# Attention scores in four groups of 32 array rows, and the best logit subtracted once instead of per tile

## The chip, the cores and the metric

The kernel runs on one core of one Trainium2 chip. The metric is device time in microseconds (us) of one execution. TensorE (PE) multiplies matrices, VectorE (DVE) and ScalarE (ACT) read its results from PSUM, GpSimd (POOL) works on SBUF and issues indirect DMAs, and SyncE (SP) issues the other DMAs. The engines run side by side and wait for each other by semaphores.

## The reference, cut to what matters

Two layers work on x of shape (2, 1024, 256) in float32. Each is an attention over a context of 77 rows, then a feed-forward part with experts. Both attentions have 16 heads of depth 16. In layer 0 the router keeps the four best of 32 experts for a token, and weights them by a softmax over their logits:

```python
q = _split_heads(x @ Wq.T) * DEPTH ** (-0.5)
k = _split_heads(y @ Wk.T)
v = _split_heads(y @ Wv.T)
logits = jnp.einsum('bhqd,bhkd->bhqk', q, k) + bias
weights = jax.nn.softmax(logits, axis=-1)
attn = jnp.einsum('bhqk,bhkd->bhqd', weights, v)
...
logits = flat.astype(jnp.float32) @ router_w.T + router_bias
scores = jax.nn.softmax(logits, axis=-1)
topk_scores, topk_idx = jax.lax.top_k(scores, TOPK)
topk_scores = topk_scores / jnp.clip(topk_scores.sum(axis=-1, keepdims=True), 1e-12, None)
```

In layer 1 a mask takes the place of the bias, there are biases on q, k, v and the output, and the router takes the one best of 8 experts.

## The kernel before, in words

The 2048 tokens are 16 tiles of 128. Each layer goes through an attention stage (one pipelined loop over the tiles, with the router of the same layer woven in) and an expert stage. Layer 0 has a shared expert between them (12 tiles after the attention, the other four inside layer 1's attention), then 95 gathered tiles of 128 rows (`experts0`); layer 1 has 23 gathered tiles (`experts1`).

The attention loop is written out by hand. Every engine has its own function `step(t)` for t from -5 on, and a step handles several tiles at different depths: `on(t, 2)` guards the work on tile t+2, and so on. On PE a step (`step0`, `step1`) is, in layer 0: transpose the first half of the softmax numerators (`transpose_p`, L885), router logits of tile t-2 (L907), output projection of tile t-1 (L914), turn the normalised rows of tile t+2 (`rows_turned`, L900), the other transposes (L885, L892, L893), the queries of tile t+2 (L923), the weighted values of tile t (`weigh`, L937: ten blocks, 51 columns each), **the scores of tile t+2 (`scores`, L950)**, turn the router's rows (L959), turn the attention's output (L966). A float32 matmul of the program appears in the trace as two LDWEIGHTS and two MATMULs. Layer 1 has the same parts in another order.

`scores` makes the logits of 16 heads against 77 context rows. The keys lie block-diagonal in `kbd`: a group of 64 array rows holds 4 heads of 16 rows, against 4 x 77 = 308 columns, so that one matmul with 64 rows (half the array) makes 4 heads. Four matmuls, g = 0 to 3, go to banks 0 to 3; g even uses rows 0 to 63 and g odd rows 64 to 127. `kbd` is filled on DVE (`keys`, L1433) from the keys times `mask_k`.

DVE's order in a step is written by hand as well. For layer 0: add the router's bias (L1535), maximum over the keys for heads 8 to 15 of tile t+1 (`maxima`, L1497), the 8 best logits of tile t-2 (`dve.max`, L1543), residual add (L1506), their indices (L1553), statistics for two layer norms (L1397), **the four best logits minus the best into `wgt` (L1565)**, mean and variance (L1402), indices to float (`ef`, L1579), one-hot of the four experts of tile t-3 and two sums (`chosen0`, L1458, L1462, L1464), epsilon (L1406), reciprocal of the softmax sum (L1597), normalised output (`o_sb`, L1599), the two layer norms (`xr`, `xn`, L1410), four additions of the bias to the scores in banks 0 to 3 (L1626), maxima of heads 0 to 7 (L1497). In layer 1 four multiply-adds that combine layer 0's expert rows (`combine`, L1488) stand in between, and L1565 and `chosen0` do not exist; L1574, L1584 and L1609 rank the tokens of an expert.

POOL in a step computes 1/sqrt for both norms (L585, L590); in layer 0 it subtracts the maxima from a whole tile of scores (L609), in layer 1 it gathers expert rows (L597) and adds the output bias (L604). ACT copies transposes to SBUF (L683, L720, L721, L708, L698, L743), scales the queries (L726, L730) and takes the exponentials (L736 for a whole tile in layer 0, L691 head by head in layer 1). Behind `experts0` ACT takes the exponential of all of `wgt` (L807) after a wait on the semaphore `RT["below"]`. `keep_busy` (L844) issues matmuls on ones that nobody reads.

```python
for g in range(NG):
    pe.wait_ge(T["q"], n + 3)
    if g % 2 == 0:
        need(pe, T["copied"], 2 * n + 3 + g // 2)
...
    dve.tensor_scalar(wgt[:, bass.ds((t - 2) * TOPK, TOPK)], m8[w][:, 0:TOPK], m8[w][:, 0:1],
                      None, ALU.subtract).then_inc(RT["below"], 1)
```

Of the kernel before, what the change touches and what calls it, by code (L numbers as in the profile page):

```python
# [22 lines left out]
P = 128  # L23
# [10 lines left out]
HG = 4  # L34
NG = H // HG
PC = (H * S2 + P - 1) // P
LASTROWS = H * S2 - (PC - 1) * P
# [20 lines left out]
NOH = NT  # L58
TEMP_END = 9276
VF_BACK = 632  # L60


def need(eng, sem, n):

    if not isinstance(n, int) or n > 0:
        eng.wait_ge(sem, n)
# [13 lines left out]
def build(nc, A):  # L80
    ctx = ExitStack()
    with ctx:
# [6 lines left out]
        def cut(region, at, shape, dt=F32):  # L89

            n = int(np.prod(shape))
            words = n if dt in (F32, I32, U32) else (n + 1) // 2
            v = region[:, at:at + words]
            if dt != F32:
                v = v.bitcast(dt)
            if len(shape) > 1:
                names = "abcd"[:len(shape)]
                v = v.rearrange(f"p ({' '.join(names)}) -> p {' '.join(names)}",
                                **dict(zip(names, shape)))
            return v, at + words  # L100
# [25 lines left out]
        kbd, vbd, bias = [None, None], [None, None], [None, None]  # L126
        kbd[0], o = cut(R2, o, (B * KC, HG, S2))
        vbd[0], o = cut(R2, o, (B * PC, 3 * VC))
# [6 lines left out]
        for name in ("Wq", "Wk", "Wv", "Wo"):  # L135
            attn_w[1][name], o = cut(U, o, (KC, D))
        kbd[1], o = cut(U, o, (B * KC, HG, S2))
        vbd[1], o = cut(U, o, (B * PC, 3 * VC))
# [84 lines left out]
        own_e, tile_less, tok_1 = route1[:, 0:E1], route1[:, E1:E1 + PLAN1], route1[:, E1 + PLAN1:]  # L223
        mask_k = sb("mask_k", [P, HG])
        mask_v = sb("mask_v", [P, PC, 3])
# [20 lines left out]
        lg = sb("lg", [P, E0])  # L246
        m8 = [sb(f"m8_{i}", [P, 8]) for i in range(2)]
        i8 = [sb(f"i8_{i}", [P, 8], U32) for i in range(2)]
        ef = sb("ef", [P, NT * TOPK])
# [414 lines left out]
        def _(act):  # L664
# [140 lines left out]
            experts0_steps(act, experts0)  # L805
            act.wait_ge(RT["below"], NT)
            act.activation(wgt[:, :], wgt[:, :], ACT.Exp).then_inc(R0["exp"], 1)  # L807
# [31 lines left out]
        def _(pe):  # L839
# [35 lines left out]
            def attention(l):  # L875
# [66 lines left out]
                def scores(t, n):  # L942

                    for g in range(NG):
                        pe.wait_ge(T["q"], n + 3)
                        if g % 2 == 0:
                            need(pe, T["copied"], 2 * n + 3 + g // 2)
                        c, half = g // 2, g % 2
                        r = slice(64 * half, 64 * half + 64)
                        mm = pe.matmul(bank[g][:, 0:HG * S2], qT[r, c, :],  # L950
                                       kbd[l][r, batch(t, 2) * KC + c].rearrange("p h k -> p (h k)"),
                                       start=True, stop=True)
                        if half:
                            mm.then_inc(T["sc_mm"], 1)

# [436 lines left out]
        def _(dve):  # L1392
# [29 lines left out]
            def keys(l):  # L1422
                K = KV
                dve.wait_ge(consts_in, 16 * CONSTS)
                for m in range(KC):
                    dve.wait_ge(K["k_mm"], 2 * KC if l else m + 1)
                    if m:
                        dve.wait_ge(K["k_bd"], B * (KC * l + m))
                    dve.tensor_scalar(k_sb, kv_k[l][m], bqk[:, 1, m:m + 1] if l else 0.0, None,
                                      ALU.add).then_inc(K["k_sb"], 1)  # L1430
                    dve.wait_ge(K["k_sb"], KC * l + m + 1)
                    for b in range(B):
                        dve.tensor_tensor(kbd[l][:, b * KC + m],  # L1433
                                          k_sb[:, b * S2:(b + 1) * S2].unsqueeze(1).to_broadcast([P, HG, S2]),
                                          mask_k[:, :].unsqueeze(2).to_broadcast([P, HG, S2]),
                                          ALU.mult).then_inc(K["k_bd"], 1)
# [29 lines left out]
            def attention(l):  # L1466
# [41 lines left out]
                def step(t):  # L1508
# [3 lines left out]
                    ne, nk = (E0, E1)[l], (TOPK, 1)[l]  # L1512
                    w, m = par(-2), n - 1
                    if l == 0 and isinstance(t, int) and t == -2:
                        keys(0)
                        dve.tensor_copy(iota16[:, :], iota[:, :])
                        dve.wait_ge(bias_in[0], 32)
                        dve.wait_ge(route_in[0], 32)
# [21 lines left out]
                    if on(t, -2):  # L1540

                        wait_apart(dve, RT["lg"], m)
                        dve.max(m8[w][:, :], lg[:, 0:ne]).then_inc(RT["mx"], 1)  # L1543
                    if l == 1 and on(t, -3):
# [6 lines left out]
                    if on(t, -2):  # L1551
                        wait_apart(dve, RT["mx"], m)
                        dve.max_index(i8[w][:, :], m8[w][:, :], lg[:, 0:ne]).then_inc(RT["ix"], 1)  # L1553
                    if l == 1 and on(t, 3):
# [4 lines left out]
                    if on(t, 3):  # L1559
                        if l == 1:  # L1560
                            wait_apart(dve, TL["x_comb"], t + 4)
                        row_stats(T, par(3), t + 3)
                    if l == 0 and on(t, -2):

                        dve.tensor_scalar(wgt[:, bass.ds((t - 2) * TOPK, TOPK)], m8[w][:, 0:TOPK], m8[w][:, 0:1],  # L1565
                                          None, ALU.subtract).then_inc(RT["below"], 1)
                    if on(t, -1):
# [3 lines left out]
                    if l == 1 and on(t, -3):  # L1571

                        dve.wait_ge(TL["rank"], t - 2)
                        dve.scalar_tensor_tensor(out=slot[:, bass.ds(t - 3, 1)], in0=ef[:, bass.ds(t - 3, 1)],  # L1574
                                                 scalar=float(N), in1=rk[:, 0:1], op0=ALU.mult,
                                                 op1=ALU.add).then_inc(TL["slot"], 1)
                    if on(t, -2):
                        dve.wait_ge(RT["ix"], m)
                        dve.tensor_copy(ef[:, bass.ds((t - 2) * nk, nk)], i8[w][:, 0:nk]).then_inc(RT["ef"], 1)  # L1579
                    if l == 0 and on(t, -3):  # L1580
                        chosen0(t - 3)
                    if l == 1 and on(t, -2):
# [383 lines left out]
            def experts0(s):  # L1966
                u = par(0)
                if isinstance(s, int) and s == 0:

                    dve.wait_ge(bias_in[1], 16)  # L1970
                    dve.tensor_scalar(bias[1], bias[1].bitcast(I32), 0.0, MASKED, ALU.is_equal,
                                      ALU.mult).then_inc(KV["mask"], 1)
# [48 lines left out]
def constants():  # L2021
# [4 lines left out]
        "ident": np.eye(P, dtype=np.float32),  # L2026
        "mask_k": ((p[:, None] % 64) // DH == np.arange(HG)).astype(np.float32),
        "mask_v": ((f // S2)[:, :, None] == (np.array(HEAD0)[None, :, None] + np.arange(3))).astype(np.float32)
# [53 lines left out]
```

## Time and profile before

| | |
|---|---|
| median of 3 runs | 785.07 us (783.95 to 786.47) |
| profiled execution | 784.07 us, its span 782.2 us (1.87 us lie around the span) |
| busy in the span | PE 729.4, PE weight loads 592.1, DVE 457.4, ACT 324.7, POOL 306.5 us |
| mean granted PE clock | 0.981 |
| attention of layer 0 | about 16 to 159 us |
| shared expert, experts0 | about 160 to 435 us |
| attention of layer 1 | about 435 to 590 us |
| experts1 | from about 597 us |

Times in a row are us from the span's start unless marked ns. In a row of a timeline, "x8" merges eight instructions of a line; the brackets at the end give how long the engine sat idle before it and who ended that. PEld is the weight load of PE, which overlaps its matmuls. The clock 1.00 is 2.4 GHz and 0.50 is 1.2 GHz.

### The profile page before, as it was taken

Reading aid. Unit: us, or ns where it says so; the run is one execution under the profiler, and the core shown is the slowest. Engines: PE = TensorE matmul, PEld = TensorE weight load, DVE = VectorE, ACT = ScalarE, POOL = GpSimd, SP = SyncE. Lnnn points to the kernel's source line nnn. Section 1 sums busy time; section 2 is a strip of 40 time slices with the busy share of each in tenths; the row PEclk is TensorE's granted clock in tenths of the full one; section 3 lists DMA queues with packets and bytes.
Section 4 is the critical chain, followed back from the end, with each engine's and each line's share of the span. In section 5 each row is a group of like instructions: output and inputs, shape, how many; then the busy total and the mean of one; then the engine's idle time right before and its main releaser. Section 6 shows DMA issues by size and latency. Waiting matters only on the chain.

```text
span 782.2 us, 15464 instructions
## 1 busy us (share of the span) xinstructions
PE 729.4 (93%) x4576; PEld 592.1 (76%) x4577; DVE 457.4 (58%) x1697; ACT 324.7 (42%) x1000; POOL 306.5 (39%) x331
## 2 busy tenths in 40 slices
PE   8799999999998999999999799988997999999994
PEld 4578888856665888888875488777774999999993
DVE  2689999647973544444433779999984232232331
ACT  1345555422221455555543488877850212212210
POOL 1243443300022555555514667763113244344421
PEclk9999999899999999999999999999998999999998
DMA  7423433340014455555872236776521565555530
GB/s 208 150 95 97 141 108 127 109 128 21 14 54 88 140 160 162 163 163 161 135 128 68 68 92 184 218 202 177 154 68 52 188 201 162 194 196 162 196 130 5
DMA packets 64181, 103.05 MB, mean 132 GB/s; under 512 B 20145, under 2 KB 42113, under 8 KB 63860
## 3 DMA queue, kind: packets, MB, share of 16 engines
q1 hardware_dynamic: 52852, 72.88, 29.9%
q0 software_dynamic: 10976, 27.22, 14.1%
q10 hardware_dynamic: 288, 2.10, 0.8%
q8 instruction: 39, 0.64, 0.3%
q14 instruction: 26, 0.21, 0.1%
HBM read 82.83 MB, written 22.07 MB: 134 GB/s over the span
## 4 chain that ended last, share of the span: by engine, by line
PE 64%; DVE 27%; DMA 3%; issue 2%; ACT 2%; POOL 1%; SPq 0%; DVEq 0%; ACTq 0%; POOLq 0%
PE bank L1368 11%; PE bank L1383 10%; PE bank L1316 9%; PE bank L937 5%; DVE U L1626 5%; PE bank L1329 5%; PE bank L1240 4%; DVE mx L1497 3%; DVE X L1488 2%; PE bank L844 2%; PE bank L1307 2%; PE bank L1288 2%; PE bank L923 2%; DMA expert_out<-U 2%; DVE R L1856 2%
## 5 line engine op out<-in xcount | busy, mean ns | idle before, releaser
L622 POOL DMA_INDIRECT U<-normed,idx_all x95 | 90.3, 951 | 141.8 <-PE bank L1307 73.7
L1316 PE MATMUL bank<-R,U 128*128 x380 | 99.2, 384 | 0.1
L1368 PE MATMUL bank<-X,R 128*128 128x128 f32 x736 | 85.9, 275 | 0.0
L1368 PEld LDWEIGHTS bank<-X,R 128*128 128x128 f32 x736 | 84.1, 192 | 0.1
L1383 PE MATMUL bank<-R,X 128*128 (+1 forms) x368 | 83.1, 379 | 0.0
L1977 DVE TENSOR_TENSOR U<-U,bank 128x128 f32<-128x128 f32 x95 | 27.3, 287 | 83.0 <-ACT U L804 82.9
L597 POOL DMA_INDIRECT R<-expert_out,slot x64 | 61.5, 960 | 35.1 <-DMA expert_out<-xr 17.7
L1383 PEld LDWEIGHTS bank<-R,X 128*128 128x128 f32 x368 | 68.2, 190 | 8.4
L691 ACT ACTIVATE U<-U,mx 128x77 f32<-128x77 f32 x256 | 67.3, 352 | 12.6 <-DVE mx L1497 12.6
L1316 PEld LDWEIGHTS bank<-R,U 128*128 128x128 f32 x380 | 65.4, 192 | 5.6 <-issue 0.3
L609 POOL TENSOR_TENSOR U<-U,mx 128x1232 f32<-128x1232 f32 x16 | 36.0, 2249 | 68.9 <-DVE mx L1497 68.9
L2005 DVE TENSOR_SCALAR X<-bank,U 128x128 f32<-128x128 f32 x92 | 25.9, 344 | 62.0 <-PE bank L1368 44.3
L648 POOL DMA_INDIRECT out<-U,idx_all x23 | 23.7, 1028 | 90.7 <-DVE U L2016 85.9
L1329 PE MATMUL bank<-R,U 128*128 x190 | 57.3, 385 | 0.1
L800 ACT ACTIVATE U<-bank 128x128 f32<-128x128 f32 x95 | 26.3, 277 | 60.7 <-PE bank L1323 60.7
L585 POOL TENSOR_TENSOR rstd<-ve,neg_half 128x1 f32<-128x1 f32 x32 | 18.1, 565 | 82.2 <-DVE ve L1406 82.2
L1497 DVE TENSOR_REDUCE mx<-U 128x8 f32<-128x616 f32 x64 | 49.9, 783 | 0.0
L820 ACT ACTIVATE X<-bank 128x256 f32<-128x256 f32 x23 | 8.8, 383 | 94.3 <-PE bank L1357 94.3
L796 ACT ACTIVATE U<-bank 128x256 f32<-128x256 f32 x95 | 36.4, 383 | 22.3 <-PE bank L1307 22.3
L1240 PE MATMUL bank<-R,xT 128*128 128x512 f32 x96 | 45.1, 593 | 0.0
L885 PE MATMUL bank<-ident,U 128*128 128x128 f32 x248 | 39.1, 283 | 4.5 <-ACT U L736 4.2
L683 ACT ACTIVATE U<-bank 128x512 f32<-128x512 f32 x62 | 36.9, 598 | 14.4 <-PE bank L885 11.5
(255 smaller groups left out, 1541.2 us busy)
## 6 DMA issues: line engine op xcount, KB each, us to landing
R<-in_w SPq DMA_DIRECT2D x21, 1024.0 KB
R<-in_w SPq DMA_DIRECT2D x40, 256.0 KB
R<-in_gu SPq DMA_DIRECT2D x8, 1024.0 KB, 5.8
expert_out<-U SPq DMA_DIRECT2D x48, 128.0 KB
expert_out<-xr SPq DMA_DIRECT2D x47, 128.0 KB
normed<-xr SPq DMA_DIRECT2D x32, 128.0 KB, 3.1
R<-in_down SPq DMA_DIRECT2D x8, 512.0 KB, 3.6
x<-X SPq DMA_DIRECT2D x16, 128.0 KB
```

Of the source, the lines that this page charges most:

```text
L597: pool.indirect_dma_start(yg[:, (i % NYG) * TOPK + j, :], None, y_d, bass.IndirectOffsetOnAxis(slot[:, a:a + 1], 0)).then_inc(TL["gath"][i ...
L622: pool.indirect_dma_start(xg0[i % NXG], None, xn_d[0], bass.IndirectOffsetOnAxis(idx_all[:, i:i + 1], 0)).then_inc(EX[0]["gath"][i % NXG], 16)
L691: ins = act.activation(sc[u][:, h * S2:(h + 1) * S2], sc[u][:, h * S2:(h + 1) * S2], ACT.Exp, bias=mx[u][:, h:h + 1])
L885: mm = pe.transpose(bank[5 + g][:, (c % 4) * P:(c % 4 + 1) * P], sc[u][:, c * P:(c + 1) * P], ident[:, :])
L937: mm = pe.matmul(bank[7][:, HEAD0[c] * VC:HEAD0[c] * VC + cols], pT[0:rows, c, :], vbd[l][0:rows, batch(t, 0) * PC + c, 0:cols], start=(c ...
L1240: mm = pe.matmul(bank[2 * v + a][:, :], xT_[:, c, :], sgu_w[:, c, a * FS:(a + 1) * FS], start=(c == 0), stop=(c == KC - 1))
L1316: mm = pe.matmul(bank[2 + u][:, 0:2 * F0], xgT0[u][:, c, :], gu_w[:, c, bass.ds(e, 1), :].rearrange("p a n -> p (a n)"), start=(c == 0), s ...
L1329: pe.matmul(bank[6 + u][:, 0:D], hT0[u], down_w[:, bass.ds(e, 1), :].rearrange("p a n -> p (a n)"), start=True, stop=True).then_inc(X0["dn ...
L1368: mm = pe.matmul(bank[1 + 2 * v + f // 4][:, (f % 4) * P:(f % 4 + 1) * P], w1_of[v][:, c, f * P:(f + 1) * P], xgT1[v][:, c, :], start=(c = ...
L1383: mm = pe.matmul(bank[6 + u][:, 0:D], hT1[u][:, c, :], w2_w[:, bass.ds(e, 1), c, :].rearrange("p a n -> p (a n)"), start=(c == 0), stop=(c ...
L1497: dve.tensor_reduce(mx[u][:, 8 * g:8 * g + 8], s3[:, 8 * g:8 * g + 8, :], AX.X, ALU.max, negate=(l == 1)).then_inc(T["mx"], 1)
L1626: ins = dve.tensor_tensor(s3[:, HG * q:HG * q + HG, :], bank[q][:, 0:HG * S2].rearrange("p (h k) -> p h k", h=HG), bt.to_broadcast([P, HG, ...
```

## The change

The scores of a tile are made by eight matmuls with 32 array rows each instead of four with 64. A group of 32 rows holds two heads, against 2 x 77 = 154 columns. The eight go in two rounds (c = 0, 1) of four groups (g = 0 to 3); group g writes bank g, round c its half of the 308 columns. Both increments of `sc_mm` now come in the last round. The rows of Wq and Wk (and their biases) are permuted on the host so that banks hold the same heads as before; `kbd` and `mask_k` have half the columns. `wgt` is no longer made tile by tile: `dve.max` of layer 0 writes into a buffer for all tiles (`best0`), and one subtraction over all 16 tiles stands at step 0 of `experts0`. In DVE's step `chosen0` stands ahead of the conversion of the indices.

```diff
+QH, QR = HG // KC, P // NG
...
-        kbd[0], o = cut(R2, o, (B * KC, HG, S2))
+        kbd[0], o = cut(R2, o, (B * KC, QH, S2))
...
+        best0 = sb("best0", [P, NT, 8])
...
-            act.wait_ge(RT["below"], NT)
+            act.wait_ge(RT["below"], 1)
             act.activation(wgt[:, :], wgt[:, :], ACT.Exp).then_inc(R0["exp"], 1)
...
-                    for g in range(NG):
-                        pe.wait_ge(T["q"], n + 3)
-                        if g % 2 == 0:
-                            need(pe, T["copied"], 2 * n + 3 + g // 2)
-                        c, half = g // 2, g % 2
-                        r = slice(64 * half, 64 * half + 64)
-                        mm = pe.matmul(bank[g][:, 0:HG * S2], qT[r, c, :],
-                                       kbd[l][r, batch(t, 2) * KC + c].rearrange("p h k -> p (h k)"),
-                                       start=True, stop=True)
-                        if half:
-                            mm.then_inc(T["sc_mm"], 1)
+                    pe.wait_ge(T["q"], n + 3)
+                    for c in range(KC):
+                        for g in range(NG):
+                            if c == 0 and g % 2 == 0:
+                                need(pe, T["copied"], 2 * n + 3 + g // 2)
+                            r = slice(QR * g, QR * g + QR)
+                            mm = pe.matmul(bank[g][:, c * QH * S2:(c + 1) * QH * S2], qT[r, c, :],
+                                           kbd[l][r, batch(t, 2) * KC + c].rearrange("p h k -> p (h k)"),
+                                           start=True, stop=True)
+                            if c == KC - 1 and g % 2:
+                                mm.then_inc(T["sc_mm"], 1)
...
+                    best = best0[:, min(max(t - 2, 0), NT - 1), :] if l == 0 else m8[w][:, :]
...
-                        dve.max(m8[w][:, :], lg[:, 0:ne]).then_inc(RT["mx"], 1)
+                        dve.max(best, lg[:, 0:ne]).then_inc(RT["mx"], 1)
...
-                    if l == 0 and on(t, -2):
-
-                        dve.tensor_scalar(wgt[:, bass.ds((t - 2) * TOPK, TOPK)], m8[w][:, 0:TOPK], m8[w][:, 0:1],
-                                          None, ALU.subtract).then_inc(RT["below"], 1)
...
+                    if l == 0 and on(t, -3):
+                        chosen0(t - 3)
                     if on(t, -2):
                         dve.wait_ge(RT["ix"], m)
                         dve.tensor_copy(ef[:, bass.ds((t - 2) * nk, nk)], i8[w][:, 0:nk]).then_inc(RT["ef"], 1)
-                    if l == 0 and on(t, -3):
-                        chosen0(t - 3)
...
                 if isinstance(s, int) and s == 0:

+                    dve.wait_ge(RT["mx"], NT)
+                    dve.tensor_tensor(wgt[:, :].rearrange("p (t j) -> p t j", t=NT), best0[:, :, 0:TOPK],
+                                      best0[:, :, 0:1].to_broadcast([P, NT, TOPK]), ALU.subtract).then_inc(RT["below"], 1)
...
-        "mask_k": ((p[:, None] % 64) // DH == np.arange(HG)).astype(np.float32),
+        "mask_k": ((p[:, None] % QR) // DH == np.arange(QH)).astype(np.float32),
```

## Rows read from the trace of the kernel before

**Rows 1.** The chain of waits in layer 0: start, us, engine and line.
```profile
87.80 0.44 PE bank L900 x2
...
93.43 1.54 DVE U L1626 x4
...
95.83 0.44 PE bank L900 x2
...
145.20 1.44 DVE wgt L1565
```

**Rows 2.** The timeline of one steady tile of layer 0.
```profile
88.53 2.25 POOL L609 TENSOR_TENSOR U<-U,mx 128x1232 f32<-128x1232 f32 x1 [3.71 <-DVE mx L1497]
...
89.61 1.19 DVE L1565 TENSOR_SCALAR wgt<-m 128x4 f32<-128x4 f32 x1
...
91.96 1.31 PE L950 MATMUL bank<-R,qT 64*128 64x308 f32 x8
92.07 0.26 DVE L1597 RECIPROCAL rs<-bank 128x16 f32<-128x16 f32 x1 [0.31 <-PE bank L937]
...
93.20 0.44 PE L959 MATMUL bank<-ident,xr 128*128 128x128 f32 x2
```

**Rows 3.** Busy in layer 1's attention: PE, PEld, DVE, ACT, POOL, clock, DMA, GB/s.
```profile
470.00:560.00 90.00, 82.69 (x633) 69.91 (x632) 88.51 (x339) 71.75 (x256) 51.92 (x65) 1.00 0.66 190
```

**Rows 4.** L950 alone in slices of that tile: slice, its length, PE (x) and PEld (x).
```profile
91.95:91.97 0.02, 0.01 (x2) 0.01 (x2) 1.00 0.00 0
91.97:92.30 0.33, 0.33 (x2) 0.29 (x4) 1.00 0.00 0
```

**Rows 5.** The view and columns of rows 3, two stretches at the end of layer 0's attention.
```profile
144.80:148.10 3.30, 2.38 (x20) 2.26 (x20) 3.18 (x11) 1.64 (x4) 2.35 (x2) 1.00 0.54 218
148.20:155.00 6.80, 6.31 (x26) 5.82 (x27) 2.47 (x14) 2.25 (x6) 0.00 (x0) 0.50 0.45 135
```

**Rows 6.** The timeline at the start of layer 1's attention.
```profile
445.24 2.43 PE L950 MATMUL bank<-U,qT 64*128 64x308 f32 x8 [3.78 <-ACT qT L730]
...
447.60 3.66 PE L844 MATMUL bank<-ones 128*128 128x512 bf16 x14
...
456.17 0.26 DVE L1597 RECIPROCAL rs<-bank 128x16 f32<-128x16 f32 x1 [3.87 <-PE bank L937]
```

**Rows 7.** The timeline at the last scores of layer 1.
```profile
569.27 1.31 PE L950 MATMUL bank<-U,qT 64*128 64x308 f32 x8
...
569.67 0.42 DVE L1599 TENSOR_TENSOR o_sb<-bank,rs 128x256 f32<-128x256 f32 x1
...
570.51 0.44 PE L966 MATMUL bank<-ident,o_sb 128*128 128x128 f32 x2
...
573.60 0.17 DVE L1529 TENSOR_TENSOR U<-bank,U 128x8 f32<-128x8 f32 x1 [0.86 <-PE bank L914]
```

**Rows 8.** The timeline at the end of layer 0's attention.
```profile
145.12 1.52 DVE L1565 TENSOR_SCALAR wgt<-m 128x4 f32<-128x4 f32 x1
...
148.69 0.69 PE L959 MATMUL bank<-ident,xr 128*128 128x128 f32 x2 [1.51 <-DVE xr L1410]
...
151.17 2.05 PE L914 MATMUL bank<-R,oT 128*128 128x256 f32 x4
...
161.45 0.21 DVE L1565 TENSOR_SCALAR wgt<-m 128x4 f32<-128x4 f32 x1
```

**Rows 9.** The timeline of a steady tile of layer 1.
```profile
483.43 1.11 PE L914 MATMUL bank<-U,oT 128*128 128x256 f32 x4
...
484.76 0.16 DVE L1529 TENSOR_TENSOR U<-bank,U 128x8 f32<-128x8 f32 x1
...
487.42 0.74 POOL L604 TENSOR_TENSOR X<-X,U 128x256 f32<-128x256 f32 x1
...
487.88 0.32 DVE L1574 SCALAR_TENSOR_TENSOR slot<-ef,rk 128x1 int32<-128x1 f32 x1
```

**Rows 10.** The page: the costliest groups of instructions.
```profile
L1977 DVE TENSOR_TENSOR U<-U,bank 128x128 f32<-128x128 f32 x95 | 27.3, 287 | 83.0 <-ACT U L804 82.9
```

More of the change, by code:

```diff
@@ L58 @@
 NOH = NT
-TEMP_END = 9276
+TEMP_END = 8660
 VF_BACK = 632
@@ L136, in build @@
             attn_w[1][name], o = cut(U, o, (KC, D))
-        kbd[1], o = cut(U, o, (B * KC, HG, S2))
+        kbd[1], o = cut(U, o, (B * KC, QH, S2))
         vbd[1], o = cut(U, o, (B * PC, 3 * VC))
@@ L223, in build @@
         own_e, tile_less, tok_1 = route1[:, 0:E1], route1[:, E1:E1 + PLAN1], route1[:, E1 + PLAN1:]
-        mask_k = sb("mask_k", [P, HG])
+        mask_k = sb("mask_k", [P, QH])
         mask_v = sb("mask_v", [P, PC, 3])
@@ L1433, in keys @@
                         dve.tensor_tensor(kbd[l][:, b * KC + m],
-                                          k_sb[:, b * S2:(b + 1) * S2].unsqueeze(1).to_broadcast([P, HG, S2]),
-                                          mask_k[:, :].unsqueeze(2).to_broadcast([P, HG, S2]),
+                                          k_sb[:, b * S2:(b + 1) * S2].unsqueeze(1).to_broadcast([P, QH, S2]),
+                                          mask_k[:, :].unsqueeze(2).to_broadcast([P, QH, S2]),
                                           ALU.mult).then_inc(K["k_bd"], 1)
@@ L1552, in step @@
                         wait_apart(dve, RT["mx"], m)
-                        dve.max_index(i8[w][:, :], m8[w][:, :], lg[:, 0:ne]).then_inc(RT["ix"], 1)
+                        dve.max_index(i8[w][:, :], best, lg[:, 0:ne]).then_inc(RT["ix"], 1)
                     if l == 1 and on(t, 3):
@@ L2052 @@
     arrays["ctxT"] = rows_of(a["ctx_1024"].reshape(B * S2, D).T)
+    rows = np.arange(D).reshape(NG, KC, QH * DH).swapaxes(0, 1).reshape(D)
     for l in range(2):
         for w in ("Wq", "Wk", "Wv", "Wo"):
-            arrays[f"L{l}_{w}"] = rows_of(a[f"L{l}_xattn_{w}"].T)
+            m = a[f"L{l}_xattn_{w}"]
+            arrays[f"L{l}_{w}"] = rows_of((m[rows] if w in ("Wq", "Wk") else m).T)
     arrays["bias0"] = rows_of(a["fside_1x1xSxS2_0"].reshape(S, S2))
     arrays["mask1"] = rows_of(a["mask_BxSxS2_if1"].reshape(N, S2))
-    arrays["bqk"] = np.stack([a["L1_xattn_bq"].reshape(KC, P).T, a["L1_xattn_bk"].reshape(KC, P).T], 1)
+    arrays["bqk"] = np.stack([a["L1_xattn_bq"][rows].reshape(KC, P).T, a["L1_xattn_bk"][rows].reshape(KC, P).T], 1)
     arrays["bv"] = a["L1_xattn_bv"].reshape(1, D)
```

## The prediction

> **What bounds the kernel now.** The change touches three things: PE's scores (L950), a small subtraction on DVE (L1565), and the place of a conversion. Whether their time counts depends on the stage, so I read the chain of waits first, then the timeline around each place.
>
> In the attention of layer 0 a tile takes 95.83 - 87.80 = 8.03 us, and two engines share it in series [rows 1]. PE has it from its turned rows at 87.80 to the end of the weighted values at about 92.04. DVE has it from its reciprocal at 92.07 [rows 2] to 95.8: output, two norms, four additions to the scores (93.43), the maxima, the router's bias, which frees PE again. The scores are on neither half. They start at 91.96, behind the values, and PE then idles until DVE has made `xr`, so that L959 starts only at 93.20 [rows 2]. In PE's half DVE has 0.31 us to spare ahead of its reciprocal, although L1565 takes 1.19 us there [rows 2]. In layer 1's steady tiles DVE is busy 88.51 us of 90 and the chain runs on DVE alone [rows 3].
>
> **Scores on PE.** One tile is eight trace matmuls in 1.31 us [rows 2]. They go in pairs, one per row group: in the first 0.02 us two weight loads and two matmuls start, and then no further matmul until 92.30 [rows 4]. From the first start, 0.36 us pass to the second pair; four pairs and the run-out fill 1.31, so a later pair takes about 0.26 us, which fits 308 columns. A weight load of 128 columns goes at 2.26/20 = 0.113 us when they follow each other over all rows [rows 5]. After the change there are sixteen matmuls of 154 columns in four rounds of four. If the four groups overlap as the two do now, a round costs the larger of 0.13 (half of 0.26) and 0.113 us: an estimate of 0.10 (first load) + 4 x 0.13 + 0.26 (run-out) = 0.8 to 0.9 us, that is 0.5 us less for PE in a tile. From below: with no overlap beyond today's two groups it would stay at 1.3; with loads one behind the other it is dearer (a rival below).
>
> The Trainium skill ("TensorE: Matmul & The Clock Gate", Part 3) says that weight loads overlap running matmuls only where the row group differs, and that four 32-row groups gave 3.07 times the speed of one; on its rule the sixteen would end within my estimate. The trace agrees for two groups [rows 4], and no row shows four.
>
> What do the 0.5 us bring? In layer 0's steady tiles nothing: PE waits for `xr` anyway. Both releases of DVE's additions now come with the last round, at about 91.96 + 0.85 = 92.8, still ahead of the first addition at 93.4 [rows 1]. In layer 1's steady tiles nothing, for DVE is the chain. Two tiles are different.
> - The second scores of layer 1 (445.24) take 2.43 us against 1.31, as at half clock; 14 `keep_busy` matmuls of 3.66 us follow and then the first transposes [rows 6]. Half clock doubles my rounds: 0.1 + 4 x 0.26 + 0.1 = 1.2 us, so PE is 1.2 us earlier. Of that, keep-busy matmuls give back 0.4, because I estimate that two more of them fall into the half-clock time (14 took 3.66 us, 0.26 each over both clocks). DVE idles 3.87 us in front of the first reciprocal (456.17), so the shift reaches it: **-0.75** (bounds 0 and -1.2).
> - The last scores (569.27) hold up L966, whose input is there at 569.67 + 0.42 = 570.09, but which starts at 570.51. PE is the bound from there, since DVE idles 0.86 us for it at 573.60 [rows 7]: **-0.4** (bounds 0 and -0.42).
>
> The first scores of each layer are released by ACT and release DVE; their first half took 0.8 us and all of them will: 0 (bounds -0.1, +0.1). The new order waits for `copied` a little earlier, but DVE copied those banks a tile before: 0. The four multiplications of `keys` halve; they lie ahead of the first scores and off the chain: 0.
>
> **The subtraction.** L1565 costs 0.21 us where POOL is quiet (161.45) and 1.52 us at 145.12 [rows 8]. In the steady tile it ends at 89.61 + 1.19 = 90.80, and POOL's L609 ends at 88.53 + 2.25 = 90.78 [rows 2]: DVE waits there for POOL. Removing it takes 1.2 to 1.5 us of DVE time from each tile in which it meets POOL, and 0.2 from the last ones. In the steady tiles that lengthens a wait of 0.31 us that PE ends: 0. On the chain it stands once, at tile step 14: 1.44 us at 145.20 [rows 1], where no scores follow, and from there through `ve`, POOL and `xr` to L959 at 148.69, in front of which PE idled 1.51 us [rows 8].
>
> What is late next there? DVE's next operation is the one-hot of `chosen0`, moved ahead of the conversion. It has two SBUF inputs. A row says that such an operation waits for POOL too: L1574 takes 0.32 us and ends at 488.20, just after L604 at 487.42 + 0.74 = 488.16 [rows 9]. So the stall moves on to L1458, and what is left to gain is the end of L1565, L1402 and the two small ones that now run inside the wait: **-0.3**. If L1458 is not held, its three operations (0.7 us) run during POOL's and the conversion takes the stall: -0.6, the lower bound; the upper is 0.
>
> The Trainium skill ("SBUF — State Buffer", "Who interferes with whom") says that a VectorE instruction with two SBUF inputs contends with a GpSimd instruction that reads SBUF. It speaks against the move: by it the term is -0.3, without it -0.6. The row on L1574 agrees.
>
> At step 17 the subtraction is on the way to the router's counts: **-0.1**. The one subtraction in `experts0` is 64 elements wide, a fraction of a microsecond, in a stage where DVE idles 83 us in front of L1977 [rows 10]: 0, and at most +0.3 if that cover were gone. Its added wait on `RT["mx"]` is over long before, and what queues behind it (the mask, values of layer 1) is not needed at once. ACT's wait on `below` comes after `experts0`: 0.
>
> **Sum**: -0.75 - 0.4 - 0.3 - 0.1 = -1.55 us, from 784.07 to 782.5 for the profiled execution, whose time is 1.0 below the median. Against the median of 785.07: **783.5 us**, -0.2%. All bounds together give -2.4 to +0.4, so 782.7 to 785.5.
>
> **The rivals.**
> 1. *The clock falls in layer 1 (slower).* At 144.8 to 148.1 PE did 19 of the narrow matmuls of L937 and then idled, 2.38 us busy of 3.30; from 148.2 to 155.0 the granted clock was 0.50 (1.2 GHz) [rows 5]. The steady part of layer 1 held 1.00 [rows 3]. Its tiles have the same 20 narrow matmuls, then 1.31 us of wide scores, then short idle times. The scores shrink to 0.85 and the idle time grows, so this place comes nearer to the one where the clock fell. Price: behind it PE has 12 turns and transposes until L914. At half clock two took 0.69 instead of 0.44 us [rows 2, 8], so 12 lose 1.5; L914 takes 2.05 instead of 1.11 [rows 8, 9], 0.9 more. The margin ahead of DVE's L1529 is 484.76 - 484.54 = 0.2 [rows 9]. That is 2.2 us if all of it is hit, 1.4 if two thirds are. It decides from the third fall on (3 x 1.4 - 1.55 = +2.65). For three to six falls: 787.7 to 791.9, with four 789.1. Against it: PE is idle 7.3 us of 90 there already, and the clock held [rows 3]. Chance 0.20; one or two falls (784.9 to 786.3) 0.10.
> 2. *The fall at the end of layer 0 goes away (faster).* `xr` comes 0.3 to 0.6 us earlier and the idle gap of 1.51 us shrinks. If the 6.8 us of 1.2 GHz [rows 5] vanish, PE's work there (6.31 us) loses at most 3.2 us; with 2.5, as L937 is bound by weight loads, 781.0. For it: the gap sits just there. Against it: it only shrinks, and the narrow matmuls stay. Chance 0.14.
> 3. *Four groups do not load together.* Sixteen loads in series cost 16 x 0.113 = 1.8 us [rows 5], 2.05 with the run-out: DVE's additions in layer 0 would start 0.65 us later in some 15 tiles, +10 us, 793.5 and more. Rows 4 speak against it. If so, each load here is as dear as a full one. Chance 0.04.
> 4. *The edge terms come to nothing* (PE's lead is taken up by ACT at 451 or by DVE at 570): 785.1. Chance 0.06.
>
> **How the numbers follow.** The forecast has 0.46. The point from which a measurement can tell a change is 0.3%, 2.4 us, about the spread of the three runs. Faster than 782.7: rival 2 and the lower edge of my bounds, 0.26. Slower than 787.4: rivals 1 (three falls or more) and 3, 0.24. Within: 0.50. The range of 781.0 to 788.5 reaches to rival 2 and takes in one to three falls; the forecast's own is 782.7 to 785.5.
>
> **What would show it.** L950 as x16 of 154 columns in 0.8 to 0.9 us, four starts within some 0.02 us; steady tiles of 8.0 and 8.5 us as before; L1597's idle in layer 0 longer; L1458 taking about 1 us beside L609, and so DVE's busy time in layer 0 down by only about half of what L1565 took; L959 of step 14 about 0.3 us nearer to its predecessor; the clock 1.00 from 470 to 560. I am wrong if a steady tile of either layer changes by over 0.1 us, if L1458 takes 0.28 us beside L609, or if the granted clock in layer 1 shows a new fall.

## The result, and the profile after

The changed kernel takes **792.29 us** (790.06 to 797.09, four executions), the kernel before 785.46 (783.95 to 786.47, four executions): a ratio of **1.0095** with a 95% interval of **[1.0052, 1.0137]**. It is slower by 0.95%, and the interval does not reach 1. The prediction of 783.5 us is wrong, and so is its range of 781.0 to 788.5. The profiled execution took 790.06 us, its span is 788.2 us, and the mean granted clock fell from 0.981 to 0.961.

The page of the changed kernel: busy time of the engines. Most lines of the file lie two higher than before (L950 is L952 now, L966 is L968, L1458 is L1460); behind the place of L1565 some lie one lower (L1597 is L1596, L1626 is L1625).

```profile
PE 726.3 (92%) x4825; PEld 600.6 (76%) x4833; DVE 451.4 (57%) x1682; ACT 325.6 (41%) x1000; POOL 306.7 (39%) x331
```

PE and DVE are busy for 3 and 6 us less, and the time is longer. So some stretch has work that got slower or waits that got longer. First a steady tile of layer 0, from its timeline:

```profile
89.97 2.25 POOL L611 TENSOR_TENSOR U<-U,mx 128x1232 f32<-128x1232 f32 x1 [3.91 <-DVE mx L1499]
...
91.26 1.10 DVE L1460 TENSOR_TENSOR U<-iota,ef 128x128 bf16<-128x128 f32 x1
...
93.40 0.81 PE L952 MATMUL bank<-R,qT 32*128 32x154 f32 x16
...
93.50 0.26 DVE L1596 RECIPROCAL rs<-bank 128x16 f32<-128x16 f32 x1 [0.51 <-PE bank L939]
...
94.60 0.44 PE L961 MATMUL bank<-ident,xr 128*128 128x128 f32 x2 [0.39 <-DVE xr L1412]
```

It is as predicted: the scores take 0.81 us instead of 1.31, the stall beside POOL has gone from the subtraction to the one-hot (L1460 ends at 91.26 + 1.10 = 92.36, POOL at 89.97 + 2.25 = 92.22; compare [rows 2]), DVE's wait for PE is longer, and the tile takes 94.60 - 86.58 = 8.02 us from one L961 to the next, as before.

The loss is in the attention of layer 1. The starts of its scores, tile after tile, show where. This table is made from the timelines of both; a row is the time from one start to the next.

| from the 2nd scores of layer 1 | before, us | after, us |
|---|---|---|
| start of the 2nd scores | 445.24 | 442.87 |
| the next six starts, together | 51.14 (to 496.38) | 51.14 (to 494.01) |
| the next eight, one by one | 8.46, 9.23, 9.32, 9.02, 9.55, 9.15, 9.09, 9.07 | 8.59, 10.76, 9.92, 11.65, 8.32, 12.18, 8.32, 12.12 |
| those eight together | 72.89 | **81.86** |
| from the last scores to the end of the span | 212.9 | 212.3 |

-2.37 + 0 + 8.97 - 0.6 = +6.0 us: the whole difference of the two spans. (The -2.37 lies ahead of layer 1; at most 1.7 of it is a stretch of 3.4 us at clock 0.50 at 254 us, in PE's own stage, which this execution did not have.) And this is the clock, by windows: PE, PEld, DVE, ACT, POOL, clock, DMA share, GB/s. The kernel before, in the stretch of its eight tiles:

```profile
494.00:570.00 76.00, 68.07 (x523) 57.75 (x524) 74.24 (x291) 60.70 (x217) 35.73 (x47) 1.00 0.64 184
```

The changed kernel, in its own eight and over the stretch of [rows 3]:

```profile
470.00:560.00 90.00, 80.89 (x653) 72.19 (x654) 81.69 (x315) 67.12 (x233) 49.79 (x62) 0.89 0.62 180
...
494.00:576.00 82.00, 72.87 (x565) 65.76 (x567) 70.25 (x280) 59.03 (x207) 33.80 (x45) 0.83 0.56 161
```

The granted clock was 0.50 (1.2 GHz) in five stretches there: from 505.2 and 515.4 for 3.4 us, from 525.7, 546.1 and 566.6 for 6.8 us, 27.2 us in all. They cost 8.97 us, 1.8 each, or 0.33 us for each us at 1.2 GHz. By the table, the two short ones cost 1.53 and 0.60 us; the three long ones cost 6.7 us together, 2.2 each, if the shorter tile behind two of them is counted in.

**What a fall does.** A tile with one, in the timeline of the changed kernel:

```profile
546.30 1.06 PE L887 MATMUL bank<-ident,U 128*128 128x128 f32 x4
...
547.58 1.06 PE L887 MATMUL bank<-ident,U 128*128 128x128 f32 x4
...
548.53 1.00 PE L909 MATMUL bank<-rw,xrT 128*128 128x8 f32 x4
...
549.39 2.05 PE L916 MATMUL bank<-U,oT 128*128 128x256 f32 x4
...
551.55 0.17 DVE L1532 TENSOR_TENSOR U<-bank,U 128x8 f32<-128x8 f32 x1 [2.22 <-PE bank L916]
```

At 2.4 GHz these four groups take 0.60, 0.60, 0.59 and 1.11 us (the same kernel, from 487.67 on). DVE, which in the kernel before never waited for PE between 470 and 560 us ([rows 9]: L914 ended 0.2 us ahead of L1529), now waits 2.22 us for it, and that is the loss.

**What goes before one.** The first fall, at 505.2. PE and DVE in the timeline of the changed kernel:

```profile
494.01 0.81 PE L952 MATMUL bank<-U,qT 32*128 32x154 f32 x16
...
495.35 0.44 PE L968 MATMUL bank<-ident,o_sb 128*128 128x128 f32 x2 [0.53 <-DVE o_sb L1598]
...
500.25 2.42 PE L939 MATMUL bank<-U 128*128 128x51 f32 x20
...
502.60 0.81 PE L952 MATMUL bank<-U,qT 32*128 32x154 f32 x16
...
504.13 0.33 DVE L1883 TENSOR_SCALAR R<-iota,U,route 128x128 bf16<-128x128 bf16 x1
...
505.47 0.69 PE L968 MATMUL bank<-ident,o_sb 128*128 128x128 f32 x2 [2.06 <-DVE o_sb L1598]
```

The same step of the kernel before:

```profile
504.84 1.31 PE L950 MATMUL bank<-U,qT 64*128 64x308 f32 x8
507.30 0.44 PE L966 MATMUL bank<-ident,o_sb 128*128 128x128 f32 x2 [1.15 <-DVE o_sb L1599]
```

Layer 1 has two sorts of tiles. In the kernel before, a tile between 456 and 505 us is 8.46 us long or less. From the scores at 504.84 on DVE also works on the plan of `experts1` (L1884 and its neighbours, L1883 in the changed kernel), a tile takes 9.0 to 9.5 us, and PE idles longer behind its scores: 1.15 us before, and 2.06 us now. 2.42 us of narrow matmuls, 0.81 us of scores, 2.06 us of idle time: this is nearly the picture of [rows 5], ahead of the fall that the kernel before had at 148.2.

**The Trainium skill** ("TensorE: Matmul & The Clock Gate", the section on HAM oscillation) tells of gaps between the matmuls, in which TensorE waits for a DMA, as what lets the clock drop again and again in a kernel. The trace agrees in part. Here the wait is for DVE, and a gap alone does not settle it: the second fall of the changed kernel, at 515.4, comes beside a gap of 1.04 us, and the kernel before held its clock with gaps of 1.15 and 1.25. Nor is the harder sort of tile needed. A second execution of the changed kernel (e12 below) has its first fall of the steady tiles already at 499.4, beside the same gap of 0.53 us with which the one above held its clock at 495.35:

```profile
499.59 0.69 PE L968 MATMUL bank<-ident,o_sb 128*128 128x128 f32 x2 [0.53 <-DVE o_sb L1598]
```

So the picture ahead of 505.2 is one case of a fall. What decides in which tile a fall comes stays open.

### The profile page after: what moved, and what is told of

The parts are those of the page before. It is cut to its first block, busy times and chain, and to the rows that moved or that the text cites. A ratio compares the mean times of both kernels' runs of the same rounds, so it can differ in the third digit from the quotient of the medians.

```text
span 788.2 us, 15923 instructions
## 1 busy us (share of the span) xinstructions
PE 726.3 (92%) x4825; PEld 600.6 (76%) x4833; DVE 451.4 (57%) x1682; ACT 325.6 (41%) x1000; POOL 306.7 (39%) x331
## 4 chain that ended last, share of the span: by engine, by line
PE 61%; DVE 29%; DMA 2%; issue 2%; POOL 2%; ACT 2%; SPq 0%; DVEq 0%; ACTq 0%; POOLq 0%
PE bank L1370 10%; PE bank L1385 10%; PE bank L1318 10%; PE bank L1331 5%; PE bank L1242 4%; DVE U L1625 4%; DVE mx L1499 4%; PE bank L846 3%; PE bank L1309 2%; PE bank L939 2%; PE bank L1290 2%; PE bank L887 2%; DVE X L1490 2%; DVE stat L1399 2%; DVE R L1855 2%
## 5 line engine op out<-in xcount | busy, mean ns | idle before, releaser
L887 PE MATMUL bank<-ident,U 128*128 128x128 f32 x248 | 43.5, 306 | 4.9 <-ACT U L738 4.0
```

The costliest lines, as they stand in the source:

```text
L887: mm = pe.transpose(bank[5 + g][:, (c % 4) * P:(c % 4 + 1) * P], sc[u][:, c * P:(c + 1) * P], ident[:, :])
```

## The experiments

**The theories.** T1: the scores are shorter, PE works less and idles more in each tile of layer 1, and so the clock falls. T2: the form of the matmuls (32 rows, four groups) lets it fall, whatever their time. T3: the part on DVE does, or has a share. T4: the 0.95% is scatter. 18 runs were made. They fell on two kinds of chips, and this has to be told first: on kind A the kernel before takes 785.3 and 786.0 us, close to the 785.5 above; on kind B it takes 798.3 to 801.1. Each result stands beside the kernel before on its own chip.

| run | chip | median us | ratio to before [interval] | mean clock (before) |
|---|---|---|---|---|
| e12 changed | A | 794.67 | 1.0126 [1.0074, 1.0179] | 0.955 (0.974) |
| e9 changed, 4 fillers | A | 784.73 | 0.9991 [0.9964, 1.0018] | 0.977 (0.974) |
| e10 changed, 2 fillers and two edges | A | 784.26 | 0.9991 [0.9962, 1.0020] | 0.976 (0.974) |
| e11 before with the fillers of e10 | A | 784.59 | 1.0010 [0.9978, 1.0042] | 0.981 (0.974) |
| e17 before, half of layer 1's scores | A | 790.10 | 1.0065 [1.0033, 1.0098] | 0.960 (0.975) |
| e18 changed, scores twice | A | 787.27 | 1.0014 [0.9988, 1.0040] | 0.976 (0.975) |
| e5 before | B | 799.41 | 0.9981 [0.9943, 1.0018] | 0.968 (0.966) |
| e6 changed | B | 802.31 | 1.0029 [0.9997, 1.0060] | 0.952 (0.966) |
| e2, e16 changed, without the part on DVE | B | 803.96, 804.96 | 1.0055 [0.9999, 1.0110], 1.0054 [1.0023, 1.0085] | 0.949 (0.967), 0.945 (0.964) |
| e1, e15 before, with the part on DVE alone | B | 798.71, 802.09 | 0.9999 [0.9930, 1.0067], 1.0007 [0.9977, 1.0037] | 0.965 (0.967), 0.963 (0.964) |
| e4, e8 changed, 2 fillers | B | 798.39, 798.95 | 0.9999 [0.9934, 1.0063], 0.9988 [0.9952, 1.0024] | 0.964 (0.967), 0.965 (0.966) |
| e7, e14 before, half of layer 1's scores | B | 800.85, 800.88 | 1.0011 [0.9979, 1.0044], 0.9999 [0.9968, 1.0030] | 0.953 (0.966), 0.953 (0.964) |
| e3, e13 changed, scores twice | B | 827.66, 825.42 | 1.0369 [1.0306, 1.0432], 1.0308 [1.0242, 1.0374] | 0.943 (0.967), 0.947 (0.964) |

**Is it real (e12, e6).** The changed kernel once more, without an edit. e12:

> The changed kernel, unchanged, as the control of this call. T1: 0.3 to 1.0% above the kernel before, as in the two comparisons so far, with the mean granted clock 0.01 to 0.02 below that of the kernel before. T4 (scatter): a ratio of 1.000.

e6, on a chip of kind B:

> The changed kernel, unchanged, as a control on the same chip. T1 (less activity of PE in each tile of layer 1 lets the clock fall): 0.5 to 1.0% slower than the kernel before on this chip too, with three or more new stretches of 0.50 between 470 and 560 us. Rival T4 (the 1.0095 was scatter between executions, as falls come and go in either kernel): a ratio of about 1.000.

e12 has six stretches of 0.50 from 499.4 to 574.5 us, 27 us in all, and 1.0126: T4 is out on kind A. On kind B the time is 0.3% longer with an interval that takes in 1, below the 0.5 to 1.0% that T1 expected; the clock drops all the same, from 0.966 to 0.952 (on kind A from 0.974 to 0.955). So on kind B a loss of time is not shown for the whole change.

**The part on DVE alone (e1, e15), and the scores alone (e2, e16).** e1 is the kernel before with

```diff
+                    best = best0[:, min(max(t - 2, 0), NT - 1), :] if l == 0 else m8[w][:, :]
...
-                    if l == 0 and on(t, -2):
-                        dve.tensor_scalar(wgt[:, bass.ds((t - 2) * TOPK, TOPK)], m8[w][:, 0:TOPK], m8[w][:, 0:1], ...
...
+                    if l == 0 and on(t, -3):
+                        chosen0(t - 3)
...
+                    dve.tensor_tensor(wgt[:, :].rearrange("p (t j) -> p t j", t=NT), best0[:, :, 0:TOPK], ...
```

and e2 is the changed kernel with these lines undone.

> The kernel before with the part on DVE alone: best0, one subtraction in experts0, chosen0 ahead of the conversion; scores by four matmuls of 64 rows as before. T1 (the shorter scores leave PE less active in each tile of layer 1, and the granted clock falls there): the clock is 1.00 in layer 1's attention between 470 and 560 us as before; the time is that of before, less the 0.4 us of the prediction's terms for step 14 and 17, so 784.5 to 785.5. T3 (the moved stall on DVE brings the falls about): falls in layer 1 and 790 or more.

> The changed kernel with the part on DVE undone: four groups of 32 rows for the scores, the subtraction tile by tile as before. T1: the clock falls in layer 1's attention as in the changed kernel, 790 to 797. T3: no falls, about 784.

> The kernel before with the part on DVE alone. T1: the ratio to the kernel before lies at 1.000 with no stretch of 0.50 between 470 and 560 us; of the predicted 0.3 us at step 14 of layer 0 only 0.1 comes. T3 (the part on DVE has a share in the falls): a mean clock below 0.970 and 2 us or more.

> The changed kernel with the part on DVE undone. T1: all of the change's loss, 8 to 11 us more than the kernel before and a mean clock of 0.955. T3: less than half of that loss.

All four ran on kind B, where the kernel before has falls in layer 1 itself, so the absolute times of the expectations don't apply. The ratios do: the part on DVE alone makes no difference in time or clock (1.0007, 0.963 to 0.964), the scores alone give 1.0055 and 1.0054, and the clock falls to 0.949 and 0.945. T3 is out there. The part on DVE was not run alone on kind A, but e17 below has falls in layer 1 without it.

**Old form, half the time (e7, e14, e17).**

```diff
+                        wide = HG * S2 // (1, 2)[l]
-                        mm = pe.matmul(bank[g][:, 0:HG * S2], qT[r, c, :],
+                        mm = pe.matmul(bank[g][:, 0:wide], qT[r, c, :],
```

> The kernel before, with its four score matmuls of 64 rows, but in layer 1 over 154 of the 308 columns of each bank. It leaves out half of layer 1's scores (two heads of each bank). T1: PE's scores last 0.7 us instead of 1.3, as in the changed kernel, so falls of the clock appear between 470 and 560 us, and it takes as long as the changed kernel, 3 to 8 us more than the kernel before although it does less. T2 (four groups of 32 rows are the cause, not the shorter time): the time of the kernel before, or 1 us less.

> The kernel before with half of layer 1's scores left out (two heads of each bank), its matmuls over 64 rows, once more for the same reason. T1: stretches of 0.50 every 10 us between 470 and 560 us, and 5 to 10 us more than the kernel before. T2: no new stretches, the time of the kernel before or 0.5 us less.

> The kernel before with half of layer 1's scores left out (two heads of each bank), hoped for on a chip of the first kind, where the kernel before takes 785 us. T1: stretches of 0.50 every 10 us between 470 and 560 us, and 4 to 10 us more than the kernel before on such a chip. T2: the time of the kernel before or less. On a chip of the other kind (800 us): again a clock near 0.952 at an unchanged time.

**New form, twice the time (e3, e13, e18).**

```diff
-                    for c in range(KC):
+                    for c, again in ((0, 0), (0, 1), (1, 0), (1, 1)):
```

with the increments on the last of the four.

> The changed kernel with each of the eight score matmuls issued twice (a round with c=0 twice, then c=1 twice), so that PE spends about what the scores took before (1.3 to 1.5 us) in the same form of four groups of 32 rows. T1: no falls between 470 and 560, 783.5 to 786. T2 (matmuls on four groups of 32 rows do not count as activity whatever their time): the falls stay, 790 or more, and the time is above that of the changed kernel if anything.

> The changed kernel with each of its eight score matmuls issued twice, once more, since the first comparison ran on a chip with extra waits of its own in layer 1. T1 (PE's activity in a tile decides, whatever its form): no stretch of 0.50 between 470 and 560 us, a mean clock of 0.97 to 0.98 and the time of the kernel before, +0 to +1.5 us. T2 (matmuls on four groups of 32 rows don't hold the clock): falls as in the changed kernel, 0.955, and 8 to 11 us more than before.

> The changed kernel with each score matmul issued twice, hoped for on a chip of the first kind. T1: no stretch of 0.50 between 470 and 560 us, 0 to 1.5 us more than the kernel before. T2: falls as in the changed kernel, 8 to 11 us more. On a chip of the other kind: again about 25 us more, from PE's late results, which tells nothing between T1 and T2.

On kind A the pair answers T2. First e17, by lines of PE from 470 to 560 us (busy, mean ns of one | idle before) and by windows:

```profile
L951 PE MATMUL bank<-U,qT 64*128 64x154 f32 x72 | 7.2, 317 | 0.0
```

```profile
470.00:560.00 90.00, 80.92 (x580) 72.08 (x581) 82.37 (x315) 67.88 (x236) 49.62 (x62) 0.88 0.62 183
```

Then e18, the same two views:

```profile
L952 PE MATMUL bank<-U,qT 32*128 32x154 f32 x320 | 13.3, 302 | 0.0
```

```profile
470.00:560.00 90.00, 82.87 (x860) 74.17 (x859) 86.84 (x334) 70.87 (x250) 53.78 (x67) 0.98 0.64 188
```

The old form with half of its work left out is 0.65% slower than the whole, with a first fall at 505.2, the place of the changed kernel's. The new form with its work done twice is not measurably slower than before, has one fall of 3.4 us (519.5) where the changed kernel has 27 us, and stands nearer to the kernel before than the one that does it once (1.0014 against 1.0095 and 1.0126, which ran in other comparisons of kind A). So the form of the matmuls is neither needed for the falls nor enough for them, and what counts is how long the scores take: T2 is out. Two details are less clean than T1 had them. e17 has four stretches (from 505.2, 515.4, 535.9 and 556.4 us), not one every 10 us. e18 takes 1.3 us more than before, as T1 allows, but T1 had no stretch at all; its gap at 510.06 was still 1.55 us.

What these runs do not separate is the time that PE works and the time that it idles: whatever shortens the scores lengthens the gap behind them, and T1 takes the two as one.

On kind B neither tells this. e7 has a fall every 10.3 us from 471.6 to 577.4 us, as T1 says, but no loss; e3 and e13 lose 29 and 24 us, beside waits of another kind, which grow there (below).

**Give the activity back (e4, e8, e9).** In layer 1, behind the scores, k matmuls on ones into bank 4 that nobody reads; k = 2 in e4 and e8, 4 in e9:

```diff
+                    if on(t, 2) and on(t, 0):
+                        keep_busy(k, 4)
                     if t == -1:
                         keep_busy(14)
```

> The changed kernel with two keep_busy matmuls (128 rows, 512 columns, 0.43 us together at full clock) behind the scores of each tile of layer 1, where PE idles. T1: the activity that the scores lost is given back, the clock stays at 1.00 between 470 and 560, 783 to 785.5, which is not slower than before. T2: the falls have to do with the form of the scores and not with the idle time behind them, so they stay: 790 or more.

> The changed kernel with two keep_busy matmuls behind the scores of each tile of layer 1, beside its controls on one chip. T1: no new stretches of 0.50 between 470 and 560 us; the time of the kernel before or up to 1.5 us less. T2: the time of the changed kernel.

> The changed kernel with four keep_busy matmuls (0.85 us at full clock) behind the scores of each tile of layer 1 instead of two. T1 (PE's activity in a tile decides): at least as few stretches of 0.50 between 470 and 560 us as with two fillers and a mean granted clock of 0.96 to 0.98; the time of the run with two fillers or up to 1 us more, because at half clock the four take 1.7 us and then stand in front of the turn of o_sb. T2: the clock of the changed kernel, 0.95.

On kind B two fillers bring the mean clock from 0.952 (e6) to 0.965, and the ratio from 1.0029 to 0.9988; the two intervals overlap. The falls do not go away there, as T1 had expected: e4 has four and e8 has three stretches of 0.50 between 470 and 560 us, where the kernel before has two (e5) and the changed kernel five (e6). On kind A four fillers take the whole loss back: 784.73 us beside 794.67 of e12 on the same chip. By windows of e9, and in its timeline at the step that had the first fall:

```profile
470.00:560.00 90.00, 83.80 (x732) 70.97 (x741) 88.35 (x336) 70.28 (x248) 51.45 (x64) 1.00 0.64 187
```

```profile
508.15 0.44 PE L968 MATMUL bank<-ident,o_sb 128*128 128x128 f32 x2 [0.83 <-DVE o_sb L1600]
```

The work is the same in the same form, PE does 8.2 us more for nothing in these 90 us, and the time is 10 us less. That is what T1 says, and T2 does not allow it.

**A better kernel (e10, e11).** Two fillers as above and, in layer 0,

```diff
+                        if t == NT - 2:
+                            pe.wait_ge(T["copied"], 2 * NT)
+                            keep_busy(6, 0)
```

and in layer 1 `keep_busy(14)` ahead of the scores of t = -2. e11 has the same on the kernel before.

> The changed kernel with two fillers behind the scores of each tile of layer 1, 14 more ahead of the second scores of layer 1 (where PE waits 4.3 us for qT) and 6 where PE waits for xr at step 14 of layer 0. T1: the falls at about 150 us and 440 us go too, and with them some 2 us each (an execution of the kernel before lost 0.36 us for every us at 0.50): 3 to 4 us less than with two fillers alone, about 0.4% below the kernel before on this chip. Rival: the fillers stand in the way when the clock is low already and nothing is won against two fillers alone.

> The kernel before with the same fillers at the same three places. T1: its own falls at about 148 us and 445 us go, 3 to 4 us less than the kernel before; whatever the changed scores are worth in themselves shows as the difference to the changed kernel with these fillers, 0.5 to 1 us. Rival: its PE has less room behind the longer scores, so the fillers cost more than they bring: 0 to 3 us more than before.

The fillers of `keep_busy(14)` missed the place that they were meant for: the scores of t = -2 are the first of layer 1, and PE's long wait is ahead of the second. In e10:

```profile
436.35 0.81 PE L952 MATMUL bank<-U,qT 32*128 32x154 f32 x16
...
443.02 1.41 PE L952 MATMUL bank<-U,qT 32*128 32x154 f32 x16 [3.86 <-ACT qT L732]
```

So that fall stayed in both. The one at 150 us did go, in both: in e11 the steps behind it take 153.88 - 147.32 = 6.56 us between two L959, where the kernel before takes 158.09 - 148.69 = 9.40. But single executions of e11 reach from 780.5 to 790.9 us, as falls come and go elsewhere, and no ratio is under 1 by more than its interval. e10 still has one fall of 6.8 us in the steady tiles (534.7), e11 has none. No version beats the kernel before measurably, and the 3 to 4 us that were expected did not show.

**The kernel before on kind B (e5).**

> The kernel before, unchanged, as a control with its own trace: the last comparison ran on a chip where the kernel before took 798 us instead of 785, and its cause in layer 1 is open. If this chip is like the first one: 784 to 787 and no clock of 0.50 between 470 and 560 us. If it is like the second: about 798, with waits in layer 1's attention whose end PE's records do not explain.

This chip is the second case of the expectation. From the second to the last scores of layer 1 it takes 582.41 - 445.42 = 137.0 us instead of 124.0, which is the whole difference of the spans (795.2 and 782.2). An example is e3, with the scores issued twice, on the other chip of kind B. In its timeline, "remote" stands for a semaphore that came when no recorded instruction ended:

```profile
459.81 1.33 PE L952 MATMUL bank<-U,qT 32*128 32x154 f32 x32
...
464.74 0.48 DVE L1625 TENSOR_TENSOR U<-bank,U 128x308 f32<-128x308 f32 x1 [3.68 <-remote]
464.84 0.38 ACT L745 ACTIVATE oT<-bank 128x256 f32<-128x256 f32 x1 [3.14 <-remote]
```

By the record the scores ended at 459.81 + 1.33 = 461.14. DVE starts on them at 464.74, 3.6 us later, and ACT gets a result of PE only then too. Such waits, nearly all in layer 1's attention, sum to 14 us in e1, 13 in e5 and 43 in e3, where PE issues more instructions. The profiled executions of kind A have none. The reason is open: nothing was tried against it. The kernel before falls to 0.50 in layer 1 too there (at 485.1 and 498.8 in e5). That the changed kernel's falls cost less on kind B because these waits set the pace already is an argument, and was not shown.

## Why the prediction was wrong, point by point

- **The step that failed: "In layer 1's steady tiles nothing, for DVE is the chain", a term of 0.** It held for six tiles to a hundredth (51.14 us in both) and cost 8.97 us in the next eight. The mechanism was rival 1, "the clock falls in layer 1", with a chance of 0.20. Its place and its cause (shorter scores, longer idle time behind the narrow matmuls) were as written; the experiments show the shorter scores as the cause, and leave open what picks the tile.
- **Why it got only 0.20.** The argument against it was "PE is idle 7.3 us of 90 there already, and the clock held [rows 3]". That row is a mean over two sorts of tiles, and the steady tile read in [rows 9] was of the easier one. A look at the tiles from 504.84 on, with 1.15 us of idle time ahead of L966, would have put 1.15 + 0.5 = 1.65 us beside the 1.51 of [rows 8], where the clock did fall. It was 2.06. That would have been a warning and no more, for e12 fell beside a gap of 0.53 us. (The stretch of [rows 5] held 20 of the narrow matmuls, not 19.)
- **Its price was too low.** 1.4 us per fall, taken as two thirds of 2.2; measured 8.97 / 5 = 1.8. The three that lasted 6.8 us cost the full 2.2 each, the two of 3.4 us about 1.1 each. Five at 1.4 would have given 790.5; it was 792.3.
- **The range** ended at 788.5, "one to three falls", although the rival itself named six. With a cause that repeats in each tile, three is not a natural end.
- **The scores**: 0.8 to 0.9 us forecast, 0.81 measured. The Trainium skill ("TensorE: Matmul & The Clock Gate", Part 3) has four groups at 3.07 times one; no run here has one group alone; this case shows four against two, 1.31 / 0.81 = 1.6 times as fast for the same scores. Rival 3 fell.
- **The second scores of layer 1, -0.75**: nothing came. From them to the first reciprocal it is 453.77 - 442.87 = 10.90 us, before 456.17 - 445.24 = 10.93. The scores take 1.41 us instead of 2.43, but the low clock lasted 6.8 us instead of 3.4, and the keep-busy matmuls took 4.24 us instead of 3.66 [rows 6]. The estimate of 1.2 us for these scores had also put the run-out at 0.1 us, where the one for full clock has 0.26; with 0.26 it is 1.4, as measured.
- **The last scores, -0.4**: right in kind. L968 starts 576.75 - 576.69 = 0.06 us after its input, not 0.42. From the end of `o_sb` to DVE's next wait it is 3.25 us instead of 3.51, so -0.26.

The timeline of the changed kernel for the last two points:

```profile
442.87 1.41 PE L952 MATMUL bank<-U,qT 32*128 32x154 f32 x16 [4.29 <-ACT qT L732]
444.61 4.24 PE L846 MATMUL bank<-ones 128*128 128x512 bf16 x13 [0.33 <-issue]
...
453.77 0.26 DVE L1596 RECIPROCAL rs<-bank 128x16 f32<-128x16 f32 x1 [3.85 <-PE bank L939]
...
576.27 0.42 DVE L1598 TENSOR_TENSOR o_sb<-bank,rs 128x256 f32<-128x256 f32 x1
...
576.75 0.44 PE L968 MATMUL bank<-ident,o_sb 128*128 128x128 f32 x2
...
579.94 0.17 DVE L1532 TENSOR_TENSOR U<-bank,U 128x8 f32<-128x8 f32 x1 [0.61 <-PE bank L916]
```

- **The stall of L1565**: right. DVE by lines in layer 0's attention (16 to 160 us), after:

```profile
L1460 DVE TENSOR_TENSOR U<-iota,ef 128x128 bf16<-128x128 f32 x13 | 14.1, 1083 | 0.0
```

and before:

```profile
L1565 DVE TENSOR_SCALAR wgt<-m 128x4 f32<-128x4 f32 x14 | 16.4, 1168 | 0.0
...
L1458 DVE TENSOR_TENSOR U<-iota,ef 128x128 bf16<-128x128 f32 x13 | 3.6, 279 | 0.0
```

  Of the 16.4 us removed, the one-hot took back 10.5. DVE's busy time is down by 5.9 us and nothing waits for it. At step 14 the gain was 0.1, not 0.3: from L959 of the step ahead 7.36 us before (7.36 in e5), 7.27 after (7.27 in e6), 7.24 in e1. The term was mis-sized, since the one-hot at 146.76 took 1.42 us: `chosen0` ended 148.44 + 0.17 - 142.72 = 5.89 us behind L961 of the step ahead, before 147.22 + 0.17 - 141.33 = 6.06.
- **Rival 2** (the fall at the end of layer 0 goes away) did not happen: 148.2 for 6.8 us before, 150.2 for 3.4 after, with the gap still 1.38 us ahead of L961 (149.99). The shorter stretch is not the change's doing: the kernel before has 3.4 us there in e5, and the changed kernel with two fillers has 6.8 in e8. **Rival 4** was right for one of the two edges, and the clock outweighed both.

## What to carry to other kernels

Work on TensorE that is off the critical path can still keep up its clock. Before making it shorter, look at single tiles and not at the mean, find those in which TensorE idles longest, and ask what happens if all behind them runs at half speed. Where TensorE has a known idle slot, a few matmuls that nobody reads can hold the clock: four here brought 10 us back, and those of e11, in the kernel before, neither won nor lost measurably. And a time for a kernel that depends on the clock needs its own control on the same chip.

## What the runs showed that was not expected

- Doing a matmul twice made the kernel faster than doing it once (1.0014 against 1.0126 times the kernel before, each on its own chip of kind A), and leaving half of the scores out made the kernel before slower (1.0065).
- A us at 1.2 GHz costs less than half a us where another engine sets the pace. A line through single executions (time over the us at 0.50, worked out as twice the missing share of the clock times the span) has a slope of 0.34 over 25 executions of the kernel before on one chip of kind A, 0.36 over 41 on one of kind B; the eight tiles gave 0.33. The other larger sets of the kernel before give 0.42 (19 executions beside e17) and 0.29 (25 beside e13), so the figure is rough.
- The falls are not tied to a place: 25 executions of the kernel before on the chip of e9 to e12 had mean clocks from 0.965 to 0.979, and times from 782.1 to 791.5 us. Time and clock go together there (correlation 0.94 with the us at 0.50), so most of the scatter of this kernel goes with the clock.
- On some chips the same kernel takes 13 us more, in one stage, with results of PE that come up to several us behind its records. Its cause is open.
